# Grouped attention: values held stationary on four column strips, probabilities moving, mask as a VectorE product

## The chip, the cores and the metric

One Trainium2 chip; the program runs on one of its cores. The metric is the device time of one execution in microseconds (us), as the median of several runs. Engines are named as in the profile: PE is TensorE's matmuls and PEld its weight loads, DVE VectorE, ACT ScalarE, POOL GpSimd.

## The reference, cut to what matters

The program is a stack of feed-forward and attention layers over `x` of 8 sequences with 256 tokens and 128 channels. The change touches the second layer alone, which is two grouped attentions one after the other, a global (causal) and a local one (a window of 32 tokens), each with 16 heads of 8 channels and 4 key/value heads:

```python
def repeat_kv(x):
    return jnp.repeat(x, H // KVH, axis=1)
def sdpa(q, k, v, mask):
    scores = jnp.einsum('bhqd,bhkd->bhqk', q, k) / np.sqrt(HD).astype(np.float32)
    scores = jnp.where(mask, scores, jnp.float32(-1e+30))
    probs = jax.nn.softmax(scores, axis=-1)
    return jnp.einsum('bhqk,bhkd->bhqd', probs, v)
```

In front of it stand an RMS norm, the projections, a rotation of q and k by position and a norm of each q and k; behind it the output projection and the residual.

## The kernel before

`grouped_attention(nc, m, tag, local)` (L1145) is called twice, with tags `global` and `local`. One **unit** `n` is one sequence of 256 tokens, kept as two tiles (`PAIR`) of 128 tokens on the partitions. `threaded` (L1133) runs the eight units; each engine's queue is written out by hand in its own `unit(u, n, prev, next)`, which loops over eight **groups** `g` of two heads, and at set groups puts in a step of the unit before (`prev`, its end) or of the unit after (`next`, its start). `u` is the parity of the unit. All four queues run in order, and semaphores join them.

The steps of a unit's start, which the unit before threads through its groups:

- DVE `start_a` (L1373): statistics of the RMS norm (helper lines L109 to L119); POOL `norm_power` (L140): the power -1/2; DVE `start_b` (L1376, helper line L130): scaling.
- PE `start_a` (L1204): two transposes (L1207); ACT `start_b` (L1322): the copy to `xT`; PE `start_b`, `start_c` (L1210, L1219) with ACT `start_c` between them in the global case: the projections.
- DVE `start_d` (L1379): values to `va` (L1384), the rotation, squares and their sums (to L1397); ACT `start_d` (L1331): Ln and Exp of them; DVE `start_d2` (L1399): the norm of q and k, written as pieces of a split so that float32r products keep precision (L1403 to L1415).
- PE `start_d` (L1227): ten transposes (L1231, L1233), those of k into the bank `ps_o`; ACT `start_e` (L1337): two copies to `qT`; DVE `start_e` (L1418): the copy to `kT`.

Per group: PE `scores` (L1236) computes transposed scores of two heads into one of two buffers, keys on the partitions, queries along the free axis, as 128 x 384 columns (256 queries of the first key tile, 128 of the second; local 160 and 128). The two heads sit on different strips of 32 rows. The mask is added by a product of the identity with -30000 where masked (L1243 local, L1245 global). ACT `exps` (L1343) takes the exponentials into `pT`, which has four buffers. PE `values` (L1249) uses each head's `pT` as stationary and the values with a column of ones as moving:

```python
nc.tensor.matmul(ps_av(0, slot), p[:, 0:P], v(0), start=True, stop=True)
nc.tensor.matmul(ps_av(1, slot), p[:, W0:W], v(1), start=True, stop=local)
last = nc.tensor.matmul(ps_av(1, slot)[0:Q1, :], p[:, P:W0], v(0), start=False, stop=True, skip_group_check=local)
```

A float32 product is two records in the trace, each with its weight load. `Q1` is 128 in the global case and 32 in the local one, where L1257 is a tile of 128x32.

The end of a unit: DVE `end_a` (L1422) divides by the sums (L1424, L1427); PE `end_a` (L1262) turns the result (L1265), ACT `end_b` (L1347) copies it (L1349), PE `end_b` (L1268) projects it (L1271), DVE `end_c` (L1433) adds the residual (L1435; local also the statistics of the next norm, L109 to L121), and in the local case `residual_end` scales.

Of the kernel before, what the change touches and what calls it, by code (L numbers as in the profile page):

```python
# [17 lines left out]
P = 128  # L18
D = 128
NB = 8  # L20
SEQ = 256
# [1123 lines left out]
def grouped_attention(nc, m, tag, local):  # L1145
# [11 lines left out]
    VW = HD + 1  # L1157

    STREAM = SEQ - (HEADS - 1) * VW
    VPAD = (KV - 1) * VW + STREAM
    w = m.a0l if local else m.a0g
    src = m.H1 if local else m.XN
    with ExitStack() as ctx:
# [14 lines left out]
        ident16, hidden = (ctx.enter_context(nc.sbuf_tensor(f"{tag}_{k}", [P, w], mybir.dt.bfloat16)) for k, w in (("ident16", P), ("hidden", W)))  # L1180
        qT = sbr("qT", [P, 2, 4, SEQ])
        kT = sbr("kT", [P, 2, SEQ])
        va = sb("va", [P, 2, PAIR, VPAD])
        pT = sb("pT", [P, 4, 2, W])
        rec = sb("rec", [P, PAIR * HEADS])
        o = sb("o", [P, PAIR, HEADS, HD])
# [5 lines left out]
        s_ready, e_ready, av_ready, o_ready, otr_ready, oT_ready, y_ready = (sem(k) for k in ("s_ready", "e_ready", "av_ready", "o_ready", "otr_ready", "oT_ready", "y_ready"))  # L1192
        ps_s = lambda g: m.psum[:, 2 * (g % 2):2 * (g % 2) + 2, :]
        ps_a, ps_b = m.psum[:, 4, 0:SEQ], m.psum[:, 5, 0:PAIR * 192].rearrange("p (t f) -> p t f", t=PAIR)
        ps_av = lambda t, slot: m.psum[:, 6, 256 * t + slot * VW:256 * t + slot * VW + STREAM]
        av_heads = m.psum[:, 6, :].rearrange("p (t f) -> p t f", t=PAIR)[:, :, 0:HEADS * VW].rearrange("p t (s f) -> p t s f", f=VW)
        ps_o = m.psum[:, 7, 0:SEQ]
        ps_y = m.psum[:, 7, 256:512]
# [4 lines left out]
        def _(pe):  # L1203
# [23 lines left out]
            def start_d(u, n):  # L1227
                pe.wait_ge(qk_ready, n + 1)
                for t in range(PAIR):
# [3 lines left out]
                    last = nc.tensor.transpose(ps_o[:, t * P:(t + 1) * P], ks[:, t, :, :].rearrange("p h f -> p (h f)").bitcast(F32), m.ident[:, :])  # L1233
                last.then_inc(qkT_ready, 1)

            def scores(u, n, g):  # L1236
                for k, (kv, j) in enumerate(heads_of(g)):
                    rows = slice(4 * HD * kv, 4 * HD * (kv + 1))
                    nc.tensor.matmul(ps_s(g)[:, k, 0:W0], kT[rows, u, 0:P], qT[rows, u, j, 0:W0], start=True, stop=True)
                    nc.tensor.matmul(ps_s(g)[:, k, W0:W], kT[rows, u, P:SEQ], qT[rows, u, j, P:SEQ], start=False, stop=True, skip_group_check=True)  # L1240
                for k in range(2):
                    if local:
                        last = nc.tensor.matmul(ps_s(g)[:, k, 0:W], ident16[:, :], hidden[:, 0:W], start=False, stop=True, skip_group_check=True)  # L1243
                    else:
# [4 lines left out]
            def values(u, n, g):  # L1249
# [9 lines left out]
                if g == GROUPS - 1:  # L1259
                    last.then_inc(av_ready, 1)  # L1260
# [1044 lines left out]
```

## Time and profile before

| | us |
|---|---|
| median of 3 runs (2650.71 to 2653.58) | 2651.41 |
| the profiled execution | 2654.27 |
| its span in the profile | 2652.5 |
| busy in the span: PE 2233.1, PEld 1855.7, DVE 1509.7, ACT 1003.5, POOL 131.7 | |

Busy time is the union of an engine's instructions; matmuls are pipelined, so a record of one lasts longer than it keeps the next one waiting. Times in the rows are counted from the start of the span. "Idle before" in square brackets is how long the engine had waited, and for what. The granted clock (PEclk) is the share of TensorE's full clock in a stretch.

### The profile page before, as it was taken

How to read it: one execution, taken by the hardware profiler on the slowest of the kernel's cores; microseconds unless marked ns; L12 is line 12 of the kernel's file. 1: busy time of each engine (PE TensorE's matmuls, PEld its weight loads, DVE VectorE, ACT ScalarE, POOL GpSimd, SP SyncE). 2: the span in 40 equal slices, each digit the busy share in tenths (PEclk: the TensorE clock that was granted, in tenths of full speed). 3: DMA queues.
4: the chain of work that ended last, by engine and by line, in shares of the span. 5: the costliest groups of instructions: out<-in, count | busy, mean ns of one | idle time of the engine just before them, and what ended most of it. 6: DMA issues, size and time to landing. Idle time of an engine off the chain costs nothing. (4 is left out here: it accounts for less than half of the span.)

```text
span 2652.5 us, 41991 instructions
## 1 busy us (share of the span) xinstructions
PE 2233.1 (84%) x14884; PEld 1855.7 (70%) x14884; DVE 1509.7 (57%) x3769; ACT 1003.5 (38%) x2327; POOL 131.7 (5%) x191
## 2 busy tenths in 40 slices
PE   3588789966997788499899989999989987688885
PEld 2377666645996322399899967888779984588863
DVE  6633334366666899756632226777742238577757
ACT  2233322223222332122344435555544435344434
POOL 2100000010000100100000000000000000000000
PEclk9799989987998899599989989999989999799978
DMA  5000000000000000000000004444300000000000
GB/s 155 1 1 0 0 1 0 0 28 1 1 0 1 0 0 0 32 1 0 1 1 0 0 27 133 124 124 123 123 1 0 0 1 0 1 1 0 0 0 16
DMA packets 47122, 59.70 MB, mean 23 GB/s; under 512 B 7089, under 2 KB 44689, under 8 KB 46323
## 3 DMA queue, kind: packets, MB, share of 16 engines
q1 hardware_dynamic: 47023, 58.43, 7.2%
q8 instruction: 57, 0.93, 0.1%
q14 instruction: 42, 0.34, 0.0%
HBM read 32.20 MB, written 26.21 MB: 22 GB/s over the span
## 5 line engine op out<-in xcount | busy, mean ns | idle before, releaser
L1650 ACT ACTIVATE a_p<-psum,a_nmax 128x256 f32<-128x256 f32 x256 | 100.4, 476 | 140.1 <-DVE a_nmax L1707 140.1
L701 ACT ACTIVATE m2b_hid<-psum,m_b 128x256 f32<-128x256 f32 x256 | 100.5, 475 | 115.1 <-PE psum L55 115.0
L701 ACT ACTIVATE m2a_hid<-psum,m_b 128x256 f32<-128x256 f32 x256 | 100.5, 475 | 114.4 <-PE psum L55 114.3
L1600 PE MATMUL psum<-a_va,a_pT 128*128 128x121 f32 x1024 | 134.5, 287 | 10.9 <-DVE a_pT L1711 6.4
L1600 PEld LDWEIGHTS psum<-a_va,a_pT 128*128 128x128 f32 x1024 | 124.4, 199 | 17.7 <-DVE a_pT L1711 7.1
L686 PE MATMUL psum<-m_w,m2a_hid 128*128 128x128 f32 x1024 | 126.2, 277 | 0.0
L686 PE MATMUL psum<-m_w,m2b_hid 128*128 128x128 f32 x1024 | 126.2, 277 | 0.0
L719 DVE SCALAR_TENSOR_TENSOR m2b_acc<-psum,m2b_gates,m2b_acc 128x128 f32<-128x128 f32 x128 | 39.0, 347 | 149.2 <-PE psum L686 149.2
L719 DVE SCALAR_TENSOR_TENSOR m2a_acc<-psum,m2a_gates,m2a_acc 128x128 f32<-128x128 f32 x128 | 39.0, 347 | 148.8 <-PE psum L686 148.8
L686 PEld LDWEIGHTS psum<-m_w,m2b_hid 128*128 128x128 f32 x1024 | 122.1, 194 | 0.6
L686 PEld LDWEIGHTS psum<-m_w,m2a_hid 128*128 128x128 f32 x1024 | 122.1, 194 | 0.6
L1948 ACT ACTIVATE a_p<-a_p,a_nmax 128x256 f32<-128x256 f32 x128 | 63.9, 500 | 141.9 <-DVE a_nmax L1975 141.9
L1711 DVE COPY a_pT<-psum 128x1024 f32<-128x1024 f32 x64 | 78.3, 1224 | 64.7 <-PE psum L1587 63.6
L1056 DVE TENSOR_TENSOR_SCAN a1s_clamped<-a1s_clamp_coef,a1s_bounds 128x1024 f32<-128x1024 f32 x48 | 108.8, 2269 | 0.0
L589 ACT ACTIVATE m1b_silu<-psum 88x512 f32<-88x512 f32 x80 | 47.4, 593 | 143.7 <-PE psum L55 143.7
L589 ACT ACTIVATE m1a_silu<-psum 88x512 f32<-88x512 f32 x80 | 47.4, 593 | 143.1 <-PE psum L55 143.1
L53 PE MATMUL psum<-m1a_XT_high,m_raw_high 128*88 (+1 forms) x320 | 97.8, 306 | 0.0
L53 PE MATMUL psum<-m1b_XT_high,m_raw_high 128*88 (+1 forms) x320 | 97.4, 304 | 0.0
L1901 PE MATMUL psum<-arena,a_q 128*128 128x384 f32 x256 | 93.9, 489 | 3.1 <-ACT a_kk L1961 3.1
L55 PE MATMUL psum<-m1a_XT_high,m_raw_low 128*88 (+1 forms) x320 | 91.6, 286 | 0.0
L55 PE MATMUL psum<-m1b_XT_high,m_raw_low 128*88 (+1 forms) x320 | 91.2, 285 | 0.0
L575 PE MATMUL psum<-m_down,m1b_hid 88*128 88x128 f32 x640 | 86.5, 278 | 5.4 <-DVE m1b_hid L615 4.9
(598 smaller groups left out, 6023.2 us busy)
## 6 DMA issues: line engine op xcount, KB each, us to landing
a_scratch<-a_pos SPq DMA_DIRECT2D x64, 384.0 KB, 2.7
a_shifted<-a_scratch SPq DMA_DIRECT2D x64, 256.0 KB, 3.1
m_w<-in_m_w SPq DMA_DIRECT2D x1, 2048.0 KB
arena<-in_m_w SPq DMA_DIRECT2D x1, 2048.0 KB, 8.3
arena<-in_m_up SPq DMA_DIRECT2D x1, 1760.0 KB, 7.4
a_w<-in_a_w SPq DMA_DIRECT2D x1, 1536.0 KB, 7.9
out<-X SPq DMA_DIRECT2D x1, 1024.0 KB, 5.1
m_down<-in_m_down SPq DMA_DIRECT2D x1, 880.0 KB
```

The costliest lines, as they stand in the source:

```text
L53: nc.tensor.matmul(out, lhsT[0], rhs[0], start=True, stop=False)
L55: return nc.tensor.matmul(out, lhsT[1], rhs[0], start=False, stop=True)
L575: last = nc.tensor.matmul(ps_y(e % 2)[:, t * D:(t + 1) * D], hid[:, e % 2, k * SEQ + t * P:k * SEQ + (t + 1) * P], m.m1_down[:, e, k, :], ...
L589: nc.scalar.activation(silu[:, e % 2, :], ps_up(e % 2)[:, 0:2 * SEQ], ACT.Silu).then_inc(silu_ready, 1)
L686: last = nc.tensor.matmul(ps_y(e % 2)[:, t * D:(t + 1) * D], hid[:, e % 2, c * SEQ + t * P:c * SEQ + (t + 1) * P], m.m2_w2[:, e, c, :], st ...
L701: last = nc.scalar.activation(hid[:, e % 2, c * SEQ:(c + 1) * SEQ], ps_up(e % 2)[:, c * SEQ:(c + 1) * SEQ], ACT.Gelu, bias=m.m2_b1[:, e * ...
L719: last = nc.vector.scalar_tensor_tensor(out=a, in0=ps_y(e % 2)[:, t * D:(t + 1) * D], scalar=gates[:, t, e:e + 1], in1=a, op0=ALU.mult, op ...
L1056: nc.vector.tensor_tensor_scan(flat(clamped[:, k % RING, :, :]), flat(clamp_coef[:, k // QUARTERS % 2, :, :]), flat(bounds[:, k % RING, :, ...
L1600: last = nc.tensor.matmul(ps_av(t, 2 * g + k), pT[:, g % 4, 2 * k + kt, t * P:(t + 1) * P], va[:, u, kt, h * VW:h * VW + STREAM], start=(k ...
L1650: last = nc.scalar.activation(p[:, g % 2, k, :], ps_s(g)[:, k, :], ACT.Exp, bias=nmax[:, g % 2, k:k + 1])
L1711: nc.vector.tensor_copy(pT[:, g % 4, :, :], ps_t).then_inc(pT_ready, 1)
L1901: last = nc.tensor.matmul(ps_pos[:, t, :], q2[:, t * P:(t + 1) * P], rel_k[:, h, P - P * t:P - P * t + WIN], start=True, stop=True)
```

## The change

The mask product on PE goes. In its place DVE multiplies the exponentials by a mask of ones and zeros, in place, once a group (`mask`, new). Values become stationary: for each `j` of four (two groups, so four heads, one for each key/value head) PE runs `values(u, n, j)`, in which each of the four key/value heads has a strip of 32 columns of the array, with nine of them used, and its head's `pT` moves through. The result lies transposed, so ACT copies it out (`move_values`), PE turns it back (`turn_back`), and DVE divides it (`normalise`), four times a unit. PE `values` waits for `masked` and `av_moved`, `turn_back` for `av_moved` and `o_ready` (or `y_used`), PE `start_d` also for the second normalisation of the running unit, since k's transposes and `turn_back` share a bank. ACT `start_d` moves from group 6 to 5, ACT `start_b` and `start_c` from groups 2 and 3 to 1 and 2, DVE `start_d2` from 6 to 5, PE `end_a` and `end_b` from 1 and 2 to 2 and 3, the local `residual_end` from 4 to 5. In `scores` the order of the four products changes. The casts of identity and mask in DVE's `first` go. The diff, cut to its core:

```diff
             def start_d(u, n):
                 pe.wait_ge(qk_ready, n + 1)
+                if not isinstance(n, int) or n:
+                    pe.wait_ge(o_ready, 4 * n - 2)
...
-                for k in range(2):
-                    if local:
-                        last = nc.tensor.matmul(ps_s(g)[:, k, 0:W], ident16[:, :], hidden[:, 0:W], start=False, stop=True, skip_group_check=True)
...
-            def values(u, n, g):
-                pe.wait_ge(e_ready, GROUPS * n + g + 1)
...
+            def values(u, n, j):
+                pe.wait_ge(masked, GROUPS * n + 2 * j + 2)
+                if not isinstance(n, int) or n or j > 0:
+                    pe.wait_ge(av_moved, 4 * n + j)
+                strip = lambda kv: ps_av[STRIP * kv:STRIP * (kv + 1), :]
+                p = lambda kv: pT[:, (2 * j + kv // 2) % 4, kv % 2, :]
+                for kv in range(KV):
+                    nc.tensor.matmul(strip(kv)[:, 0:W0], va[:, u, 0, kv, :], p(kv)[:, 0:W0], start=True, stop=True)
+                for kv in range(KV):
+                    last = nc.tensor.matmul(strip(kv)[:, P:SEQ], va[:, u, 1, kv, :], p(kv)[:, W0:W], start=False, stop=True, skip_group_check=True)
+                last.then_inc(av_ready, 1)
+            def turn_back(u, n, j):
+                pe.wait_ge(av_moved, 4 * n + j + 1)
+                if j:
+                    pe.wait_ge(o_ready, 4 * n + j)
+                elif not isinstance(n, int) or n:
+                    pe.wait_ge(y_used, n)
+                for t in range(PAIR):
+                    last = nc.tensor.transpose(ps_back[:, t * P:(t + 1) * P], ov[:, j % 2, t * P:(t + 1) * P], m.ident[:, :])
+                last.then_inc(back_ready, 1)
...
             def unit(u, n, prev, next):
...
+                    if g in (2, 4, 6):
+                        values(u, n, g // 2 - 1)
+                    if g == 0 and prev:
+                        values(1 - u, n - 1, 3)
                     if next and g == GROUPS - 1:
                         pe.wait_ge(e_ready, GROUPS * n + g)
                         ready(n + 1)
                         scores(1 - u, n + 1, 0)
+                    if g in (4, 5, 7):
+                        turn_back(u, n, {4: 0, 5: 1, 7: 2}[g])
                     if prev and g == 1:
+                        turn_back(1 - u, n - 1, 3)
...
+            def move_values(u, n, j):
+                act.wait_ge(av_ready, 4 * n + j + 1)
+                nc.scalar.activation(ov[:, j % 2, :], ps_av, ACT.Copy).then_inc(av_moved, 1)
             def unit(u, n, prev, next):
                 for g in range(GROUPS):
-                    if next and g == 6:
+                    if next and g == 5:
                         start_d(1 - u, n + 1)
                     if next and g == 7:
                         start_e(1 - u, n + 1)
                     exps(u, n, g)
+                    if g in (2, 4, 6):
+                        move_values(u, n, g // 2 - 1)
+                    if prev and g == 0:
+                        move_values(1 - u, n - 1, 3)
...
+            def mask(u, n, g):
+                dve.wait_ge(e_ready, GROUPS * n + g + 1)
+                if local:
+                    p, k = pT[:, g % 4, :, :], m.window_mask[:, :].unsqueeze(1).to_broadcast([P, 2, W])
+                else:
+                    p = pT[:, g % 4, :, :].rearrange("p h (b f) -> p h b f", f=P)[:, :, 0:3:2, :]
+                    k = m.causal_mask[:, :].unsqueeze(1).unsqueeze(1).to_broadcast([P, 2, 2, P])
+                nc.vector.tensor_tensor(p, p, k, ALU.mult).then_inc(masked, 1)
+            def normalise(u, n, j):
+                dve.wait_ge(back_ready, 4 * n + j + 1)
+                back = ps_back.rearrange("p (t k f) -> p t k f", t=PAIR, f=STRIP)
+                nc.vector.reciprocal(rec[:, :, :], back[:, :, :, HD])
+                nc.vector.drain()
+                nc.vector.tensor_tensor(o[:, :, :, j, :], back[:, :, :, 0:HD], rec[:, :, :].unsqueeze(3).to_broadcast([P, PAIR, KV, HD]),
+                                        ALU.mult).then_inc(o_ready, 1)
...
             def unit(u, n, prev, next):
                 for g in range(GROUPS):
+                    mask(u, n, g)
+                    if next and g == 1:
+                        start_b(1 - u, n + 1)
+                    if prev and g == 1:
+                        normalise(1 - u, n - 1, 3)
                     if next and g == 0:
                         start_a(1 - u, n + 1)
                     if prev and g == 3:
                         end_c(1 - u, n - 1)
+                    if prev and g == 5 and local:
                         residual_end(nc, dve, m, xn, n - 1)
                     if next and g == 4:
                         start_d(1 - u, n + 1)
+                    if g == 4:
+                        normalise(u, n, 0)
+                    if next and g == 5:
+                        start_d2(1 - u, n + 1)
+                    if g == 5:
+                        normalise(u, n, 1)
+                    if next and g == 7:
+                        start_e(1 - u, n + 1)
+                    if g == 7:
+                        normalise(u, n, 2)
```

## Rows read from the trace of the kernel before

**Rows 1.** Busy time by stretch, both stages: stretch, length, busy (instructions) by engine, PEclk.

```profile
136.00:325.00 189.00, 163.85 (x1354) 138.90 (x1354) 62.10 (x240) 70.82 (x116) 4.84 (x7) 0.98 0.00 1
342.00:545.00 203.00, 188.35 (x1304) 132.19 (x1302) 71.42 (x282) 57.01 (x107) 8.99 (x13) 0.97 0.00 1
```

**Rows 2.** Instructions of L140, 160 to 460 us: count, ns, first and last start.

```profile
L140 POOL TENSOR_TENSOR global_rn_inv<-global_rn_var,neg_half x6: 690/691/692, 163.9 to 282.1; 128x2 f32<-128x2 f32 x6
...
L140 POOL TENSOR_TENSOR local_xn_inv<-local_xn_var,neg_half x4: 691/691/692, 376.4 to 452.3; 128x2 f32<-128x2 f32 x4
```

**Rows 3.** Timeline of PE, global, one group: start, length, instructions merged by line.

```profile
219.01 0.39 PE L1239 MATMUL psum<-global_qT,global_kT 32*128 32x256 f32 x2
...
219.24 0.23 PE L1240 MATMUL psum<-global_qT,global_kT 32*128 32x128 f32 x2
219.40 0.39 PE L1245 MATMUL psum<-global_hidden,global_ident 128*128 128x256 bf16 x2
219.62 0.38 PE L1255 MATMUL psum<-global_va,global_pT 128*128 128x121 f32 x2
...
220.29 0.39 PE L1255 MATMUL psum<-global_va,global_pT 128*128 128x121 f32 x2
```

**Rows 4.** Timeline of PE, local: start of a head's values, and what follows it.

```profile
441.60 0.48 PE L1255 MATMUL psum<-local_va,local_pT 128*128 128x121 f32 x2
...
442.56 0.34 PE L1239 MATMUL psum<-local_qT,local_kT 32*128 32x160 f32 x2
```

**Rows 5.** Timeline of DVE, ACT and PE, global, one unit.

```profile
200.08 0.29 DVE L1403 TENSOR_TENSOR global_qn<-global_rot,global_inv 128x128 f32<-128x128 f32 x1 [0.61 <-ACT global_inv L1335]
...
202.11 0.66 PE L1231 MATMUL psum<-ident,global_qs 128*128 128x128 f32 x4 [1.75 <-DVE global_ks L1415]
...
203.46 1.09 ACT L1340 ACTIVATE global_qT<-psum 128x512 fp32r<-128x512 f32 x2 [2.70 <-PE psum L1233]
...
208.87 0.36 DVE L1424 RECIPROCAL global_rec<-psum 128x32 f32<-128x32 f32 x1 [4.98 <-PE psum L1257]
...
209.71 0.48 DVE L109 BATCH_NORM_STATS2 global_rn_stats<-XN 128x6 f32 x2
...
211.05 0.17 DVE L119 TENSOR_SCALAR global_rn_var<-global_rn_var 128x2 f32<-128x2 f32 x1
...
211.70 0.38 ACT L1349 ACTIVATE global_oT<-psum 128x256 f32<-128x256 f32 x1 [1.32 <-PE psum L1265]
...
212.56 0.44 PE L1207 MATMUL psum<-ident,global_r 128*128 128x128 f32 x2 [0.90 <-DVE global_r L130]
...
215.63 0.42 DVE L1435 TENSOR_TENSOR global_r<-psum,XN 128x256 f32<-128x256 f32 x1 [3.13 <-PE psum L1271]
...
219.48 0.22 DVE L1384 COPY global_va<-psum 128x64 f32<-128x64 f32 x1 [2.95 <-PE psum L1224]
...
221.67 0.49 DVE L1393 TENSOR_TENSOR global_tmp<-global_rot 128x320 f32<-128x320 f32 x1
...
222.79 0.18 DVE L1397 TENSOR_SCALAR global_ss<-global_ss 128x40 f32<-128x40 f32 x1
```

**Rows 6.** Groups of instructions, ACT, both stages: count, busy us, mean ns, idle before.

```profile
L1345 ACT ACTIVATE global_pT<-psum 128x768 f32<-128x768 f32 x64 | 51.1, 809 | 46.9 <-PE psum L1245 46.9
L1345 ACT ACTIVATE local_pT<-psum 128x576 f32<-128x576 f32 x64 | 41.6, 650 | 80.2 <-PE psum L1243 79.7
```

**Rows 7.** Timeline of DVE, local, first and last instruction of `end_c`.

```profile
424.82 0.42 DVE L1435 TENSOR_TENSOR local_r<-psum,arena 128x256 f32<-128x256 f32 x1 [3.74 <-PE psum L1271]
...
426.79 0.17 DVE L121 TENSOR_SCALAR local_xn_var<-local_xn_mv 128x2 f32<-128x2 f32 x1
```

**Rows 8.** Busy time by stretch, two stretches of other stages; columns as in rows 1.

```profile
842.00:893.00 51.00, 24.71 (x86) 15.18 (x86) 34.08 (x97) 15.55 (x24) 11.07 (x12) 0.73 0.00 1
1057.00:1129.00 72.00, 32.72 (x160) 30.45 (x161) 52.34 (x190) 8.57 (x15) 12.07 (x16) 0.55 0.08 30
```

**Rows 9.** Timeline of PE, global, first unit, at the lower clock.

```profile
132.49 1.12 PE L1231 MATMUL psum<-ident,global_qs 128*128 128x128 f32 x4 [6.51 <-DVE global_ks L1415]
```

More of the change, by code:

```diff
@@ L1247, in scores @@
-                last.then_inc(s_ready, 1)
-            def values(u, n, g):
-                pe.wait_ge(e_ready, GROUPS * n + g + 1)
-                for k, (kv, j) in enumerate(heads_of(g)):
-                    slot = 2 * g + k
-                    p = pT[:, g % 4, k, :]
-                    v = lambda t: va[:, u, t, kv * VW:kv * VW + STREAM]
-                    nc.tensor.matmul(ps_av(0, slot), p[:, 0:P], v(0), start=True, stop=True)
-                    nc.tensor.matmul(ps_av(1, slot), p[:, W0:W], v(1), start=True, stop=local)
-                    last = nc.tensor.matmul(ps_av(1, slot)[0:Q1, :], p[:, P:W0], v(0), start=False, stop=True,
-                                            skip_group_check=local)
-                if g == GROUPS - 1:
-                    last.then_inc(av_ready, 1)
+                for k, rows, j in heads:
+                    last = nc.tensor.matmul(ps_s(g)[:, k, W0:W], kT[rows, u, P:SEQ], qT[rows, u, j, P:SEQ], start=True, stop=True)
@@ L1312, in tail @@
             def tail(u, n):
-                values(u, n, GROUPS - 1)
+                values(u, n, 3)
+                turn_back(u, n, 3)
                 end_a(u, n)
@@ L1364, in unit, with tail @@
                     exps(u, n, g)
+                    if g in (2, 4, 6):
+                        move_values(u, n, g // 2 - 1)
+                    if prev and g == 0:
+                        move_values(1 - u, n - 1, 3)
                     if prev and g == 2:
                         end_b(1 - u, n - 1)
-                    if next and g in (2, 3):
-                        {2: start_b, 3: start_c}[g](1 - u, n + 1)
-            threaded(act, first, unit, end_b)
+                    if next and g in (1, 2):
+                        {1: start_b, 2: start_c}[g](1 - u, n + 1)
+            def tail(u, n):
+                move_values(u, n, 3)
+                end_b(u, n)
+            threaded(act, first, unit, tail)
         @block.vector
@@ L1466, in unit @@
                         end_c(1 - u, n - 1)
-                    if prev and g == 4 and local:
+                    if prev and g == 5 and local:
                         residual_end(nc, dve, m, xn, n - 1)
```

72 lines of the change are left out of this document (23 added, 49 removed).

## The prediction

> **What bounds the kernel now.** I read the stage windows first. The change touches only the two grouped attention stages; in them TensorE (PE) is busy 163.9 of 189 us and 188.4 of 203 us, VectorE (DVE) 62 and 71, ScalarE (ACT) 71 and 57, and the granted clock is 0.98 and 0.97 [rows 1]. Then the unit, which is one sequence: GpSimd's power (L140) runs once a unit, and its first and last starts give (282.1 - 163.9) / 5 = 23.6 us for global and (452.3 - 376.4) / 3 = 25.3 us for local [rows 2]. Eight units each make the stages. Then one group of PE work: two score pairs, two mask products (0.22 us together), and per head six records of values at 0.67 us (219.62 to 220.29) [rows 3]. A local head takes 0.96 us (441.60 to 442.56) although it streams less: L1257 is a 128x32 tile there, and changing the tile shape and back costs 0.29 us a head [rows 4]. So PE bounds both stages now, and DVE and ACT wait for it.
>
> **What the change takes from PE.** Per unit the masks go (8 x 0.22 = 1.8 us) and 16 heads of values (16 x 0.67 = 10.7 us global, 16 x 0.96 = 15.4 us local). It adds per unit four blocks of values and four pairs of turning transposes. A block streams, in each strip, 2 passes x 384 columns (288 local). On a strip the next record, L1240, follows L1239's 256 columns after 0.23 us (219.01 to 219.24) [rows 3], 0.87 to 0.9 ns a column: 0.67 us global and 0.50 local if the strips run side by side, 2.7 and 2.0 if in turn. These are my two ends. I take side by side: the two L1239 records of a pair, on different row strips, together last 0.39 us, what one of 256 columns lasts, and L1240 too comes as a pair [rows 3]. With the change of shape (0.1 in, 0.1 out, from the 0.29) a block is 0.87 us to the next instruction, and its end comes a tail of some 0.17 after its last column. A turning pair is that of L1207, 0.44 us [rows 5]. PE work falls from about 20 to 12.5 us a unit in global, from 23 to 10 in local.
>
> On column strips the Trainium skill ("TensorE: Matmul & The Clock Gate", Part 3, "Measured speedup vs the span model") gives a speedup of 2.38 for three column strips, not 3. By that a global block would stream an estimated 0.85 us in place of 0.67, some 0.4 us a unit more; the sum above does not use it, and no run here shows it.
>
> **What it adds elsewhere.** Each group now has a DVE product over 512 (local 576) elements. No row has this; SBUF products take 0.29 us for 128 and 0.49 for 320 elements [rows 5], 1.04 ns an element, so 0.69 (0.76). Lower end 0.49, upper end twice that. Two instructions of normalisation replace the three of L1424 and L1427, four times a unit: between 0.22 (the copy L1384) and 0.36 (L1424) each [rows 5]; I take 0.42 with the drain. ACT gets four copies 128x256 like L1349, 0.38 each [rows 5]. The casts of the identity and mask in the setup go, two instructions a stage of the size of L1384. There are no DMAs. Reordering the score pairs costs and gains nothing: the records already start strip beside strip [rows 3].
>
> **What sets the unit then.** All queues are in order, and the preparation of the next unit is threaded through them. I walked the four queues in program order with the durations of [rows 5] and some 0.04 us a handover. Now DVE and ACT fill PE's time; afterwards the unit is one chain in which nearly every step waits for another engine. Global, from exp 0 of a unit to exp 0 of the next:
> - exp 0 (0.81 [rows 6]), mask 0 (0.62, as the next instruction starts before its end), statistics 209.71 to 211.22 (1.51), power (0.69 [rows 2] and handovers), scaling (two of 128 elements, 0.48), transposes (0.44): 4.8 us;
> - ACT: exp 2, exp 3 and between them four copies (xT in front, values 0, oT, latent) of 0.4 to 0.5 each, like L1349: 3.3, at 8.1;
> - DVE: mask 3, end_c (L1435, a copy as large and their drains, 0.9), mask 4, start_d 219.48 to 222.98 (3.5): 5.7, at 13.8. start_d's input is there 1.3 us before; the masks and end_c stand in front of it;
> - ACT: Ln and Exp of the norm (L1403 waits 0.61 us for them), then exp 5 behind them: 1.4, at 15.1;
> - DVE: mask 5, start_d2 200.08 to 202.1 (2.0), normalisation 1, for which PE's start_d now waits: 3.1, at 18.3;
> - PE: ten transposes, 202.11 until L1340 starts at 203.46 (1.3), values 2: 2.2, at 20.5;
> - ACT: the copy of values 2, the two qT copies 1.09, exp 7 behind them: 2.2, at 22.7;
> - DVE: mask 7, and kT behind it: 1.1; PE: the next scores: 0.6. Total 24.4 us [rows 5].
>
> So the waits that PE's load hid are the bound next. Local is the same with exp at 0.65 [rows 6], masks of 0.76, an end_c of 2.1 us (424.82 to 426.96) [rows 7] and the residual's end in front of start_d2, but no latent copy: 25.1 us. At full clock the unit changes by +0.8 and -0.2 us: the 9 to 13 us taken from PE buy nothing. The last unit of a stage has no next one to prepare and PE closes it now; with the setup it saves 2 us global and 7 local. Seven pitches each: 7 x 0.8 - 2 + 7 x (-0.2) - 7 = -5 us.
>
> **The clock.** PE would be busy (tails included) 13.3 of 24.4 us and 11.1 of 25.1, so 55% and 44%. Stretches like that: 48% busy (24.7 of 51) with clock 0.73, 45% (32.7 of 72) with 0.55, against 0.98 at 87% [rows 1, 8]. The granted clock has two levels, 1.2 and 2.4 GHz; at the lower one four of the transposes last 1.12 us, not 0.66 [rows 5, 9]. The same walk with every PE step doubled gives 30.3 and 30.1 us a unit (+5.9, +5.0). I take 0.77 for global, by its 55% between the rows of 48% and 87% (46% of the time at the lower level: +2.7 us a unit), and 0.65 for local, between 0.55 and 0.73 (70%: +3.5): 7 x 6.2 = +43 us.
>
> The skill's rule in the same page (Part 1, "What's actually happening") is that the throttled state is the default and activity releases it. It speaks against a change that empties PE. Rows 8 agree; without it the sum would end at -5.
>
> **The sum.** 2654.3 us (the profiled execution; span 2652.5 and 1.8 around it) - 5 + 43 = 2692. That execution lies 2.9 us above the median of 2651.4, so I forecast 2690.
>
> **Rivals.**
> 1. The clock holds at the higher level: 2651.4 - 5 = 2646. For it: the gaps come one by one between dense groups, and in global PE stays over half busy. Against: rows 8.
> 2. The strips run in turn. A block takes 2.0 (1.5) us more, two of four blocks lie on the chain and one delays exp 1; the walk gives 29.9 and 28.8 us a unit, +64 us over case 1, and with a part of the clock's loss about 2745. For it: no row shows column strips beside each other. Against: the row strips.
> 3. The lower level nearly throughout: -5 + 7 x 10.9 + some 10 at the ends: 2730.
> 4. Faster: the DVE queue's load, not the handovers, sets the unit. Its place is start_d to start_d2 in groups 4 and 5: if that preparation runs beside exps 3 to 6 and not between them, 3.5 to 5.5 us a unit go, 14 x 4.5 = 63 us: about 2590. It decides once the pitch is under 23.6 and 25.3. For it: DVE's work is only 14 to 15 us a unit (62.1 / 8 or 71.4 / 8 [rows 1], and 8 masks plus 1 more). Against: exp 5 stands behind ACT's wait for start_d, and kT behind mask 7.
>
> **How the numbers follow.** Forecast 0.58 (2665 to 2725), case 1 0.12, case 2 0.10, case 3 0.05, case 4 0.15. A mask at 0.49 or 0.98 moves five steps a unit, -14 or +20 us, which is in these bounds. No change means within 0.2%, 5 us, about what can be measured. Faster: case 4 and half of case 1, 0.21; same: the rest of case 1, 0.06; slower 0.73. The range 2632 to 2740 leaves out case 4 and part of case 2.
>
> **What would show it.** Pitch by L140: 27 and 28.5 us. PE idle before its start_d transposes, DVE idle at masks 3, 5 and 7, ACT idle before exp 2 and exp 5. Clock 0.6 to 0.8 in both stages. In a block four records starting within a few ns say side by side; one after the other is case 2. I am wrong if the pitches are under 23.6 and 25.3, or the clock stays over 0.95.

## The result and the profile after

The changed kernel takes 2719.42 us (median of 4 runs, 2715.54 to 2719.59) against 2651.93 for the kernel before beside it: a ratio of 1.0256, 95% interval 1.0243 to 1.0269. It is 68 us slower; forecast were 2690 us and a range of 2632 to 2740. The profiled execution has a span of 2717.2 us, 65 more than before, and the two attention stages hold 60 of them: from the first power (L140) of a stage to the first of the next one, global lasts 244.8 us (207.1 before) and local 244.9 (222.5). Some 4 us lie behind the two stages, in work that the change does not touch (2108.2 us against 2103.8).

The stage windows, the same stretches and columns as [rows 1]:

```profile
136.00:325.00 189.00, 130.49 (x866) 78.72 (x866) 92.42 (x298) 65.18 (x124) 5.21 (x7) 0.56 0.00 0
342.00:545.00 203.00, 113.96 (x824) 75.53 (x824) 107.86 (x350) 57.52 (x120) 10.23 (x12) 0.55 0.00 0
```

TensorE's busy time fell from 163.9 to 130.5 us and from 188.4 to 114.0, and the granted clock from 0.98 and 0.97 to 0.56 and 0.55: the lower level for nearly nine tenths of the time. The unit, by the starts of L140 as in [rows 2]:

```profile
L140 POOL TENSOR_TENSOR global_rn_inv<-global_rn_var,neg_half x6: 691/691/692, 167.8 to 312.1; 128x2 f32<-128x2 f32 x6
...
L140 POOL TENSOR_TENSOR local_rn_inv<-local_rn_var,neg_half x6: 690/928/1245, 408.3 to 556.8; 128x2 f32<-128x2 f32 x6
```

That is 144.3 / 5 = 28.9 us for global and 148.5 / 5 = 29.7 us for local, in place of 23.6 and 25.3. The new operations, as groups by line (count | busy us, mean ns | idle before):

```profile
L1445 DVE TENSOR_TENSOR local_pT<-local_pT,window_mask 128x576 f32<-128x576 f32 x64 | 48.5, 758 | 69.3 <-ACT local_pT L1349 67.2 <-issue 1.7
L1445 DVE TENSOR_TENSOR global_pT<-global_pT,causal_mask 128x512 f32<-128x512 f32 x64 | 44.2, 690 | 88.2 <-ACT global_pT L1349 86.5 <-issue 1.6
...
L1248 PE MATMUL psum<-global_pT,global_va 128*32 128x256 f32 x256 | 33.7, 619 | 0.8 <-DVE global_pT L1445 0.7
...
L1353 ACT ACTIVATE global_ov<-psum 128x256 f32<-128x256 f32 x32 | 12.3, 385 | 93.0 <-PE psum L1250 93.0
...
L1452 DVE TENSOR_TENSOR global_o<-psum,global_rec 128x64 f32<-128x64 f32 x32 | 7.2, 225 | 2.4
...
L1450 DVE RECIPROCAL global_rec<-psum 128x8 f32<-128x8 f32 x32 | 6.5, 204 | 13.7 <-PE psum L1260 13.6
```

The mask takes 0.69 and 0.76 us, the copy 0.385, the two instructions of a normalisation 0.20 and 0.23. L1248's 256 records last 0.619 us each, 158 us together, in 33.7 us of busy time: more than four at once. In a block the four strips start 6 to 7 ns apart (285.856, 285.862, 285.869 and 285.876 us); they run side by side.

One unit of the global stage, from exponential 0 to the next (timeline; the rows at which the prediction's steps end, the waits that it named, and one block of values, L1248 and L1250, up to the instruction behind it):

```profile
279.66 0.81 ACT L1349 ACTIVATE global_pT<-psum 128x768 f32<-128x768 f32 x1 [1.70 <-PE psum L1238]
...
284.62 0.69 PE L1202 MATMUL psum<-ident,global_r 128*128 128x128 f32 x2 [1.09 <-DVE global_r L130]
...
285.35 0.47 ACT L1328 ACTIVATE global_xT<-psum,a0g_norm 128x256 f32<-128x256 f32 x1 [1.90 <-PE psum L1202]
...
285.86 1.08 PE L1248 MATMUL psum<-global_pT,global_va 128*32 128x256 f32 x8
...
286.71 0.65 PE L1250 MATMUL psum<-global_pT,global_va 128*32 128x128 f32 x8
...
287.29 0.69 PE L1266 MATMUL psum<-ident,global_o 128*128 128x128 f32 x2
...
289.29 1.48 ACT L1349 ACTIVATE global_pT<-psum 128x768 f32<-128x768 f32 x2
...
290.11 0.69 DVE L1445 TENSOR_TENSOR global_pT<-global_pT,causal_mask 128x512 f32<-128x512 f32 x1 [2.86 <-ACT global_pT L1349]
...
293.16 0.23 DVE L1400 COPY global_va<-psum 128x64 f32<-128x64 f32 x1 [0.52 <-PE psum L1219]
...
296.49 0.18 DVE L1413 TENSOR_SCALAR global_ss<-global_ss 128x40 f32<-128x40 f32 x1
...
296.70 0.24 ACT L1337 ACTIVATE global_inv<-global_ss 128x40 f32<-128x40 f32 x1 [1.68 <-DVE global_ss L1413]
...
297.15 1.49 ACT L1349 ACTIVATE global_pT<-psum 128x768 f32<-128x768 f32 x2
...
297.98 0.69 DVE L1445 TENSOR_TENSOR global_pT<-global_pT,causal_mask 128x512 f32<-128x512 f32 x1 [0.86 <-ACT global_pT L1349]
...
300.74 0.22 DVE L1452 TENSOR_TENSOR global_o<-psum,global_rec 128x64 f32<-128x64 f32 x1
...
301.02 1.12 PE L1228 MATMUL psum<-ident,global_qs 128*128 128x128 f32 x4 [2.33 <-DVE global_o L1452]
...
304.92 0.38 ACT L1353 ACTIVATE global_ov<-psum 128x256 f32<-128x256 f32 x1 [6.27 <-PE psum L1250]
...
307.01 0.69 DVE L1445 TENSOR_TENSOR global_pT<-global_pT,causal_mask 128x512 f32<-128x512 f32 x1 [5.45 <-ACT global_pT L1349]
...
308.91 0.81 ACT L1349 ACTIVATE global_pT<-psum 128x768 f32<-128x768 f32 x1 [1.93 <-PE psum L1238]
```

Here every step of the prediction's walk can be read. Exponential 0 starts at 279.66; the transposes of `r` end at 285.31, after 5.65 us (4.8 forecast); exponential 3, the first of the two merged at 289.29, ends at 290.1: 4.8 more (3.3); start_d ends at 296.67: 6.6 (5.7); exponential 5 near 297.96: 1.3 (1.4); normalisation 1 at 300.96: 3.0 (3.1); the ten transposes and values 2 until the copy starts at 304.92: 4.0 (2.2); exponential 7, with mask 7 at 307.01: 2.1 (2.2); kT, the scores and the next exponential 0 at 308.91: 1.9 (1.7). The fourth, fifth and seventh step, with DVE and ACT work alone, last what was forecast; the excess of 4.8 us lies in the steps that TensorE takes part in or holds up, and its four transposes of L1228 last 1.12 us, as in [rows 9], and not 0.66. In the third step DVE waits 0.52 us for the projection (L1219), so the input of start_d was not early, as forecast. In the first, mask 0 begins at 281.09, 0.62 us after the end of exponential 0, with the normalisation of values 2 ahead of it (until 280.79), which the walk does not list. The waits that the prediction named as signs are all there: TensorE 2.33 us ahead of its start_d, DVE 2.86, 0.86 and 5.45 at masks 3, 5 and 7, ACT 1.90 at the copy ahead of exponential 2 and 1.68 at the norm ahead of exponential 5.

### The profile page after: what moved, and what is told of

It reads as the page before. It is cut to its first block and busy times, and to the rows that moved or that the text cites. A ratio compares the mean times of both kernels' runs of the same rounds, so it can differ in the third digit from the quotient of the medians.

```text
span 2717.2 us, 41374 instructions
## 1 busy us (share of the span) xinstructions
PE 2173.7 (80%) x14244; PEld 1770.4 (65%) x14244; DVE 1604.7 (59%) x3973; ACT 1019.0 (38%) x2391; POOL 134.0 (5%) x191
## 5 line engine op out<-in xcount | busy, mean ns | idle before, releaser
L1445 DVE TENSOR_TENSOR global_pT<-global_pT,causal_mask 128x512 f32<-128x512 f32 x64 | 44.2, 690 | 88.2 <-ACT global_pT L1349 86.5
```

## The experiments

All stand against the kernel before, timed beside them on the same chip: its median was 2651.5 us beside runs 1 to 4, 2659.2 beside 5 to 8 and 2651.1 beside 9 to 12, so runs of different chips are compared by their ratios. Unit and clock are those of the profiled execution (in run 8 it was 8 us under the median). The unit is taken from five intervals of L140 in each stage (in the local stage three in the first row, where five give 25.6, and four in the row of run 11), the clock from the stretches 160 to 270 us (global) and 345 to 440 us (mostly local). Behind the two stages, in work that no run touches, the profiled executions differ by up to 20 us (2096.4 in run 5, 2116.9 in run 3).

| run | us | ratio to before (95%) | us a unit, global / local | clock |
|---|---|---|---|---|
| before | 2651.9 | 1 | 23.6 / 25.3 | 1.00 / 0.99 |
| after | 2719.4 | 1.0256 (1.0243 to 1.0269) | 28.9 / 29.7 | 0.59 / 0.54 |
| 1 TensorE kept busy | 2689.7 | 1.0140 (1.0112 to 1.0168) | 26.7 / 28.2 | 0.75 / 0.73 |
| 2 wait without mask | 2689.1 | 1.0135 (1.0106 to 1.0165) | 27.5 / 27.4 | 0.57 / 0.52 |
| 3 mask on TensorE | 2653.1 | 1.0010 (0.9994 to 1.0027) | 23.1 / 25.4 | 0.77 / 0.63 |
| 4 exponential 7 first | 2688.0 | 1.0136 (1.0108 to 1.0164) | 27.1 / 28.2 | 0.57 / 0.55 |
| 5 old values, VectorE mask | 2685.4 | 1.0105 (1.0086 to 1.0124) | 26.5 / 27.3 | 0.89 / 0.75 |
| 6 reordered | 2598.9 | 0.9768 (0.9752 to 0.9785) | 20.7 / 22.2 | 0.67 / 0.61 |
| 7 reordered, mask on TensorE | 2566.7 | 0.9645 (0.9626 to 0.9664) | 17.4 / 21.4 | 0.95 / 0.83 |
| 8 reordered, kept busy | 2583.6 | 0.9715 (0.9699 to 0.9731) | 18.6 / 20.0 | 0.95 / 0.86 |
| 9 before, reordered | 2619.5 | 0.9871 (0.9844 to 0.9897) | 20.2 / 22.9 | 1.00 / 1.00 |
| 10 as 7, local kept busy | 2583.2 | 0.9740 (0.9718 to 0.9763) | 17.1 / 22.9 | 0.97 / 0.75 |
| 11 as 8, power beside a normalisation | 2572.1 | 0.9697 (0.9674 to 0.9720) | 17.6 / 20.7 | 1.00 / 0.86 |
| 12 strip by strip | 2723.7 | one run | 29.1 / 29.9 | 0.52 / 0.52 |

### 1. Is it the clock? TensorE kept busy

```diff
+            def keep_busy(bank, count):
+                for _ in range(count):
+                    nc.tensor.transpose(m.psum[:, bank, 0:P], m.ident[:, :], m.ident[:, :])
...
+                    if next and g == 5:
+                        keep_busy(4, 12)
                     if g in (4, 5, 7):
                         turn_back(u, n, {4: 0, 5: 1, 7: 2}[g])
```

(the other three places alike: ahead of `start_d`, of `ready(n + 1)`, and 8 ahead of `start_a`)

> The changed kernel with 44 transposes of the identity more on TensorE in each unit (8, 12, 12 and 12 of them), whose results nothing reads, put where its queue stands waiting; nothing else is touched. At full clock 12 of them last 1.3 us, less than each of the waits they stand in (1.5 to 3.3 us in the trace). Theory A (the unit is a chain of handovers that at full clock would last 24.4 and 25.1 us, and what makes it 29.1 and 29.7 is the clock alone): clock over 0.9 in both stages in place of 0.56 and 0.55, pitch 24.4 to 25.5, so 2719 - 7 x 4.5 - 7 x 4.4 = about 2657 us (2645 to 2670). Rival B (the loss lies in the new operations and handovers themselves, the low clock only goes with it): the pitch stays over 28 us whatever the clock, 2710 us or more, since TensorE has more to do.

TensorE has more to do and the kernel is 30 us faster. The stage windows of this run:

```profile
136.00:325.00 189.00, 164.63 (x1238) 117.82 (x1235) 99.61 (x319) 70.15 (x134) 7.67 (x7) 0.72 0.00 1
345.00:560.00 215.00, 154.88 (x1234) 118.10 (x1234) 121.93 (x396) 63.66 (x135) 12.96 (x14) 0.72 0.00 0
```

The clock rose to 0.72 only, not over 0.9, so the time stopped between the two forecasts. TensorE's timeline shows where it was won and lost (line numbers of this run; L1281 are the added transposes):

```profile
229.39 0.58 PE L1236 MATMUL psum<-global_qT,global_kT 32*128 32x256 f32 x2
...
230.01 2.72 PE L1281 MATMUL psum<-ident 128*128 128x128 f32 x12
...
232.88 0.38 PE L1236 MATMUL psum<-global_qT,global_kT 32*128 32x256 f32 x2
...
233.25 1.53 PE L1281 MATMUL psum<-ident 128*128 128x128 f32 x12
...
240.74 0.39 PE L1236 MATMUL psum<-global_qT,global_kT 32*128 32x256 f32 x2 [1.88 <-DVE global_kT L1446]
...
242.31 0.40 PE L1250 MATMUL psum<-global_pT,global_va 128*32 128x128 f32 x8
242.64 0.53 PE L1236 MATMUL psum<-global_qT,global_kT 32*128 32x256 f32 x2
```

Twelve transposes at 230.01 take 2.72 us, the lower level; from 232.5 on the clock is up, the score pair L1236 goes from 0.58 to 0.38 us and the next twelve take 1.53. At 242.64, after a stretch with a wait of 1.88 us, scores, strips and one turning back, the pair is back at 0.53. In the first half of the unit TensorE's queue is full of projections, scores and strips (busy for all of the 8 us from 222 to 230) and the granted clock is 0.50 throughout. The size fits: the prediction's walk lies at 24.4 us at full clock and 30.3 at the lower one; at 0.59 that makes 24.4 + 0.82 x 5.9 = 29.2 (measured 28.9), at 0.75 it makes 27.3 (26.7); local 29.7 (29.7) and 27.8 (28.2). Theory A holds in kind, though its 2657 us needed a clock that did not come, and rival B, 2710 us or more, is out. The 30 us are what is left after GpSimd's power, which takes 1.06 to 1.17 us in 14 of this run's 16 units and 0.69 in most units of the changed kernel (see 11).

### 2 and 3. The mask: its work, or its place in the queue?

```diff
-                nc.vector.tensor_tensor(p, p, k, ALU.mult).then_inc(masked, 1)
+                dve.sem_inc(masked, 1)
```

> The changed kernel without the multiplication by the mask: VectorE waits for each exponential as it did and then only raises the signal, so the order of every queue stays. The mask is left out of the computation. Theory A (five of the eight masks, 0, 3, 4, 5 and 7, lie on the chain, 0.62 us of VectorE each): 3.1 us a unit less in both stages, 14 x 3.1 = 43: about 2676 us (2660 to 2690), the clock little changed. Rival C (VectorE's masks fill time in which it would wait anyway): 2710 to 2720 us.

(The mask is left out of the computation.) 30 us faster, not 43, and certainly not nothing. The 43 were worked out at full clock. Worked out after the run, the same walk with TensorE's steps doubled gives 1.9 and 2.7 us a unit for it, 32 us: by the walk, TensorE ends last in more places at the lower clock, and a shorter VectorE step is worth less there.

Run 3 takes the product with `hidden` back into `scores`, drops `mask` from VectorE's loop and lets the values wait for the exponentials:

```diff
-                    mask(u, n, g)
...
-                pe.wait_ge(masked, GROUPS * n + 2 * j + 2)
+                pe.wait_ge(e_ready, GROUPS * n + 2 * j + 2)
```

> The changed kernel with the mask of the kernel before: the identity times the hidden entries on TensorE ahead of the exponential, no mask in VectorE's queue; the strips, the copies, the turning back and the rest of the order stay. Theory A: not only the multiplications leave the chain (3.1 us) but also VectorE's waits for the exponentials ahead of start_d, start_d2 and the copy of kT, another 1.5 us or so at full clock; TensorE has 1.8 us a unit more and would be busy in two thirds of a unit, so the clock rises to 0.75 or more: pitch 20 to 23 us, 2719 - 14 x 7.5 = about 2615 us (2585 to 2640), faster than both kernels. Rival C (the strips and their handovers are the loss, wherever the mask stands): 2690 us or more. Rival B (only VectorE's work counts, not its place in the queue): as the run without the multiplication, about 2676.

66 us faster than the change, twice what the multiplications alone are worth. The other half is VectorE's waits for the exponentials in front of `start_d`, `start_d2` and kT together with a higher clock (0.77 and 0.63 against 0.59 and 0.54); no run separates the two. But not faster than before, which had been expected. Its windows:

```profile
160.00:270.00 110.00, 86.81 (x702) 52.71 (x702) 44.55 (x181) 45.92 (x90) 3.16 (x5) 0.77 0.00 0
345.00:440.00 95.00, 73.52 (x548) 46.60 (x546) 39.61 (x166) 31.52 (x68) 4.13 (x6) 0.63 0.00 1
```

The clock did reach 0.77 in global, but 0.63 in local, and TensorE carries more of the unit: the walk of this kernel, made after the run, is 19.7 us at full clock and 29.2 at the lower one (local 20.7 and 28.0), which at these clocks makes 24.0 and 26.1 (measured 23.1 and 25.4). The expectation had taken the clock's rise without the larger price of each step below it. Strips alone, then, leave the total as it was: by the walk, the work they save comes back as clock. In the profiled execution the two stages are 10 us shorter than before (207.6 and 212.2 us against 207.1 and 222.5), and the untouched work behind them is 13 us longer; why was not followed.

### 4. One place in one queue

```diff
-                    if next and g == 7:
-                        start_e(1 - u, n + 1)
                     exps(u, n, g)
-                    if g in (2, 4, 6):
-                        move_values(u, n, g // 2 - 1)
+                    if g in (2, 4, 7):
+                        move_values(u, n, {2: 0, 4: 1, 7: 2}[g])
+                    if next and g == 7:
+                        start_e(1 - u, n + 1)
```

> The changed kernel with one place in ScalarE's queue changed: exponential 7 goes ahead of the copy of values 2 and of the two copies of qT, in place of behind them. No instruction is added or taken. Theory A (the order of the queues sets the unit): mask 7 and behind it the copy of kT no longer wait for exponential 7; 1.8 us a unit less at full clock, so 14 x 1.8 = 25: about 2694 us (2675 to 2700). Rival C (the time lies in the operations, and another wait takes its place): 2714 to 2722 us.

2688.0 us: 1.8 and 1.5 us a unit, with the clock as low as before. The order of a queue is worth as much as the whole multiplication.

### 5. The other half alone

The kernel before with `mask` in VectorE's loop, `values` waiting for it, and no product with `hidden`; its values are the old ones.

> The kernel before with one half of the change: the mask moves from TensorE to VectorE (the same multiplication, ahead of everything else in each group, and the values wait for it), while the values stay as they were, probabilities stationary and no strips. Theory A (neither half is dear by itself; only both together empty TensorE so far that its clock falls): TensorE is still busy 18 of 24 us a unit, the clock stays over 0.9, and a walk of the queues gives 24.3 and 25.9 us a unit against 23.3 and 25.3 for the kernel before: 2651 + 7 x 1.0 + 7 x 0.6 = about 2662 us (2652 to 2685). Rival B (the multiplications on VectorE and their handovers are the loss): most of the 68 us of the change is there, 2690 us or more.

```profile
160.00:270.00 110.00, 87.51 (x647) 77.81 (x646) 55.31 (x166) 37.22 (x63) 4.41 (x4) 0.89 0.00 1
345.00:440.00 95.00, 73.56 (x414) 52.57 (x414) 49.45 (x157) 23.09 (x44) 5.53 (x6) 0.75 0.00 1
```

A ratio of 1.0105, 28 us, between the two forecasts: the mask on VectorE does cost something by itself, and the clock did not stay over 0.9 with it. The walk had 24.3 and 25.9 us a unit at full clock; measured are 26.5 and 27.3, with the clock at 0.89 and 0.75 and GpSimd's power at 1.10 us and not 0.69 (see 11). With the strips at 1.0010 the halves would add up to 30 us; together they cost 68. In the two stages of the profiled executions the mask costs 38 us, the strips save 10, and both together cost 60. So about half of the loss is there only when both halves are. By the walk they share a chain (at full clock 23.3 us a unit before, 19.7 with strips, 24.3 with the mask, 24.4 with both, in global); and they share a clock.

### 6. The same instructions in another order

The loops of the three queues are written as a list (`+` is the unit after, `-` the one before; k mask, n normalise, e exponential, m copy of values, s scores, v values, t turn back):

```diff
+TensorE: "s1 v3- s2 t3- s3 start_a+ s4 end_a- start_b+ end_b- start_c+ v0 s5 t0 v1 t1 s6 s7 start_d+ v2 scores+ t2"
+ScalarE: "e0 e1 m3- e2 start_b+ end_b- start_c+ e3 m0 start_d+ e4 m1 e5 e6 e7 start_e+ m2"
+VectorE: "start_a+ k0 start_b+ n3- k1 k2 end_c- k3 start_d+ n0 start_d2+ n1 k4 k5 residual- start_e+ k6 k7 n2"
```

> The changed kernel with the same instructions in another order on TensorE, ScalarE and VectorE: on VectorE the statistics of the next unit ahead of mask 0, its start_d right behind mask 3 and start_d2 ahead of masks 4 and 5, the copy of kT ahead of masks 6 and 7; on ScalarE exponentials 5 to 7 ahead of the copies of qT; on TensorE values later and the transposes ahead of values 2. Theory A (the order of the queues, not the work, sets the unit): a walk of the queues gives 17.1 and 18.5 us a unit at full clock and 24.3 and 23.3 with TensorE at half; with a clock of 0.7 some 21.4 us in both stages, 2719 - 7 x 7.7 - 7 x 8.3 = about 2607 us (2560 to 2640), faster than both kernels. Rival C (other waits take the place of those removed): 2680 us or more. Rival B (the new operations are the loss): 2700 or more.

A ratio of 0.9768: 129 us under the change (0.0488 of 2652) and 2.3% under the kernel before, with no instruction added or taken; the two stages of the profiled execution are 116 us shorter than the change's (373.7 us against 489.7). Windows, and L140 in the global stage:

```profile
160.00:270.00 110.00, 95.56 (x700) 59.57 (x700) 74.29 (x242) 53.23 (x100) 5.58 (x5) 0.67 0.00 0
345.00:440.00 95.00, 63.97 (x519) 44.80 (x519) 69.77 (x232) 37.28 (x79) 7.49 (x8) 0.61 0.00 0
```

```profile
L140 POOL TENSOR_TENSOR global_rn_inv<-global_rn_var,neg_half x6: 1113/1118/1122, 157.5 to 261.2; 128x2 f32<-128x2 f32 x6
```

With these clocks the walk makes 21.9 and 22.2 us (measured 20.7 and 22.2). Theory A was right in size; B and C are out.

### 7 and 8. Order and clock together

Run 7 is run 3 in such an order (values 2 and 1 earlier, no masks on VectorE).

> Strips with the mask on TensorE as in the kernel before, and the queues in an order like that of the reordered run (exponentials and values of a group later than the next unit's preparation). Theory A: a walk of the queues gives 16.7 and 18.8 us a unit at full clock, 28.1 and 26.2 with TensorE at half; since TensorE now has 14 of 17 us to do the clock should stay higher, 0.8 or more: 20 to 21.5 us a unit, 2719 - 14 x 8.5 = about 2600 us (2545 to 2640). Rival C (TensorE's work bounds again and the order buys nothing over the run with the mask on TensorE alone): 2640 to 2660.

```profile
160.00:270.00 110.00, 95.85 (x968) 61.48 (x960) 55.57 (x230) 65.32 (x122) 4.13 (x6) 0.95 0.00 1
345.00:440.00 95.00, 66.83 (x655) 45.66 (x654) 50.70 (x211) 39.04 (x84) 6.20 (x9) 0.83 0.00 0
```

2566.7 us, the fastest of the study: 3.5% under the kernel before, 6.0% under the change by the ratios. The clock is 0.95 in global, where 17.4 us a unit stand against the walk's 16.7, and 0.83 in local.

Run 8 is run 6 with transposes put into TensorE's queue (`b`, with their number; the diff is against run 6):

```diff
-"... s3 start_a+ ... v1 t1 s6 ..."
+"... s3 b6+ start_a+ ... v1 b20+ t1 s6 ..."
```

> The reordered run with 26 transposes of the identity more on TensorE in each unit, results unread: 6 ahead of the transposes of r and 20 ahead of turning back values 1, where TensorE would wait 0.8 and 3 to 4 us. Theory A (what is left over the walk at full clock is the clock): the clock rises by 0.1 or more over that of the reordered run, and the time falls by 10 to 35 us against it, towards 7 x 17.1 and 7 x 18.5 us. Rival D (at that order TensorE's own work bounds, and more of it costs): 5 us or more slower than the reordered run.

```profile
160.00:270.00 110.00, 97.75 (x947) 67.45 (x946) 83.47 (x269) 60.55 (x115) 5.58 (x5) 0.95 0.00 1
```

Useless work again buys time: the clock went from 0.67 to 0.95, and 15 us went against run 6, timed on the same chip.

### 9. The control: does order alone do it?

> The control for the reordered runs: the kernel before, its work unchanged, with its three queues reordered in the same manner (VectorE's end_a, end_c and start_d of the next unit early, ScalarE's exponentials 5 and 6 ahead of the norm, TensorE's transposes ahead of the last values). Theory A (before the change TensorE's own work bounds, so order can give back only the few us in which TensorE waits): a walk of the queues gives 19.6 and 22.9 us a unit against 23.0 and 25.1, 7 x 3.4 + 7 x 2.2 = 39 us, a ratio of 0.985 to the kernel before; the reordered forms of the change (0.965 to 0.977) stay ahead of it, because they have 8 to 13 us a unit less for TensorE. Rival E (the gain of the reordered runs is order alone, and the change adds nothing to it): a ratio of 0.975 or less. Rival F (TensorE has no gaps to give back): 0.995 to 1.005.

```profile
160.00:270.00 110.00, 110.00 (x933) 95.97 (x932) 46.28 (x178) 48.70 (x83) 3.44 (x5) 1.00 0.00 1
345.00:440.00 95.00, 95.00 (x692) 68.97 (x690) 41.96 (x168) 30.37 (x59) 5.54 (x9) 1.00 0.00 1
```

A ratio of 0.9871, as the walk said (20.2 and 22.9 us measured, 19.6 and 22.9 forecast). Rivals E and F are out. TensorE is busy for all of both stretches at full clock: this order leaves no gap that another could fill (whether another order of TensorE's own products would be shorter was not tried). The reordered change lies below it by 1 to 2.3%; that this is so because it has less for TensorE to do is argued from the work, not tried apart. So the change is worth having, once the queues are arranged for it, though the 2.3% are those of run 7, which has only the strips and leaves the mask on TensorE.

### 10 and 11. Two details

> The reordered run with the mask on TensorE, and in the local stage 24 transposes of the identity more in each unit, results unread, ahead of turning back values 1, where TensorE waits some 4 us. Theory A (in local 20.4 us a unit stand against 18.8 of the walk because the clock is lower for a third of each unit): the local clock rises from 0.83 to 0.9 or more and 5 to 12 us go: a ratio to the kernel before of about 0.961. Rival D (the transposes only delay): the same time or up to 15 us more.

```profile
345.00:440.00 95.00, 80.60 (x671) 57.24 (x670) 44.13 (x185) 33.99 (x72) 5.51 (x8) 0.75 0.00 0
```

A miss: by the ratios 25 us slower than run 7, and the local clock fell, to 0.75. Of the 25 us the profiled executions show 10 in the local stage (191.0 us against 181.0), the only one that was touched. So the outcome is rival D's in size, but its reason, that the transposes delay, is not what the trace shows:

```profile
L1311 PE MATMUL psum<-ident x168: 272/273/273, 303.1 to 441.0; 128*128 128x128 f32 x168
```

All 168 last 0.27 us, as at full clock, 24 of them take 2.78 us in each of the seven units, in a place where run 7 waits 4.8 to 5.2 us in six of the seven, and in six TensorE still waits 1.7 to 2.6 us behind them. What differs is the clock after them: in four units the lower level then lasts 13.7 to 17.1 us in a row, against 6.8 us in most units of run 7. Why, and whether that makes the 10 us, is open.

> The reordered and kept busy run with one move in VectorE's queue: the normalisation of values 3 stands between the statistics and the scaling, where mask 0 stood, and mask 0 behind the scaling. In the reordered run GpSimd's power lasted 1.11 to 1.19 us in 12 of 14 units, and 0.69 where no mask was running when it began. Theory G (GpSimd's power waits until the mask product that is already running on VectorE has ended; a normalisation, with one source in PSUM, doesn't hold it): the power lasts 0.69 us again, 0.3 to 0.5 us a unit off the chain, 4 to 6 us in all against the run it is derived from. Rival H (the power is slowed by whatever VectorE does beside it): it stays over 0.9 us, and the time stays the same.

In run 6 a mask product was already running when the power began; in run 11 a normalisation runs in that place (timelines, one unit each):

```profile
157.39 0.69 DVE L1442 TENSOR_TENSOR global_pT<-global_pT,causal_mask 128x512 f32<-128x512 f32 x1
...
157.50 1.12 POOL L140 TENSOR_TENSOR global_rn_inv<-global_rn_var,neg_half 128x2 f32<-128x2 f32 x1 [20.86 <-DVE global_rn_var L119]
...
158.66 0.48 DVE L130 TENSOR_SCALAR global_r<-XN,global_rn_inv 128x128 f32 x2 [0.58 <-POOL global_rn_inv L140]
```

```profile
157.14 0.69 POOL L140 TENSOR_TENSOR global_rn_inv<-global_rn_var,neg_half 128x2 f32<-128x2 f32 x1 [19.89 <-DVE global_rn_var L119]
...
157.87 0.48 DVE L130 TENSOR_SCALAR global_r<-XN,global_rn_inv 128x128 f32 x2 [0.26 <-POOL global_rn_inv L140]
```

The power is back at 0.69 us in every unit, and VectorE waits 0.26 us for it and not 0.58. In run 6 the power ended 0.54 us after the mask did (158.62 against 158.08); in all five slow ones of the changed kernel it was 0.55 us after. Theory G holds for the duration: the power waits for the product to end. The Trainium skill says so ("SBUF — State Buffer", "Summary: rules for kernel authors"): a VectorE instruction with two SBUF inputs and a GpSimd one that reads SBUF exclude each other, and the second to issue waits for the first to finish. The trace agrees where the power is the second; where the mask is the second it does not show the wait: a mask that began 0.13 us after a power of the changed kernel (225.86 us) lasted its 0.69 us all the same. The longer power also stands in runs 1, 4 and 5 (1.06 to 1.24 us in 14, 12 and 14 of 16 units), and part of what they cost or gained is that. For the total, 0.9697 against 0.9715, the intervals overlap: a gain of 5 us was forecast and is not established (one execution of each has 4 us less in the two stages, 342.8 against 347.1).

### 12. Strip by strip

```diff
                 for kv in range(KV):
                     nc.tensor.matmul(strip(kv)[:, 0:W0], va[:, u, 0, kv, :], p(kv)[:, 0:W0], start=True, stop=True)
-                for kv in range(KV):
                     last = nc.tensor.matmul(strip(kv)[:, P:SEQ], va[:, u, 1, kv, :], p(kv)[:, W0:W], start=False, stop=True, skip_group_check=True)
```

> The changed kernel with the eight matmuls of a block of values issued strip by strip (both passes of strip 0, then both of strip 1, and so on) in place of the first passes of all four strips and then the second. The work is the same. Theory A (strips run side by side only where neighbours in the queue are on different strips, since TensorE issues in order): only the second pass of one strip lies beside the first of the next, a block takes four first passes and one second, at the lower clock 4 x 0.43 + 0.22 = 1.9 us in place of 0.65; two blocks lie on the chain, so 2.5 us a unit or more, 2755 us or more. Rival I (a matmul that waits for its strip doesn't hold up the strips behind it): 2715 to 2725 us, the four first passes still within a few ns.

```profile
L1248 PE MATMUL psum<-global_pT,global_va 128*32 128x256 f32 x256 | 34.8, 627 | 0.8 <-DVE global_pT L1444 0.7
```

The first passes still overlap as in the changed kernel (34.8 us busy for 256 records of 0.627), 13 ns apart instead of 6 to 7, and the time is 2723.7 us, in a single run. Rival I is right, by the trace above all.

## Why the prediction was right, and where its size was off

- **What bounds it now, and what PE loses.** Right. TensorE was the bound ([rows 1]; run 9 shows it at its end). The strips run side by side, against rival 2, and the block takes 1.43 us to the next instruction at the lower level (285.86 to 287.29 above) and 0.79 at the higher one, in run 7; 0.87 was forecast:

```profile
237.51 0.64 PE L1268 MATMUL psum<-global_pT,global_va 128*32 128x256 f32 x8
...
238.30 0.39 PE L1251 MATMUL psum<-global_qT,global_kT 32*128 32x256 f32 x2
```

By the Trainium skill's speedup of 2.38 for three column strips ("TensorE: Matmul & The Clock Gate", Part 3, "Measured speedup vs the span model") a block would take an estimated 1.05 us, with 0.85 of streaming in place of 0.67. Run 7's 0.79 us does not agree with it.

- **The added operations.** Mask 0.69 and 0.76, copy 0.38, normalisation 0.43 with its two instructions, all as forecast.
- **The chain of handovers.** Right in the main (timeline above): the steps with DVE and ACT work alone within 0.1 us, and the waits as named. Two readings were off: start_d's input came 0.5 us late and not 1.3 early, and the normalisation of values 2 ahead of mask 0 was left out. Runs 4 and 6 show that it is the order: moving instructions alone gives 31 and 129 us. Rival 4, faster if the preparation runs beside the exponentials, named the right place; it needed the queues to be rearranged, which the change does not do.
- **The clock.** This is the mis-sized term. "I take 0.77 for global ... and 0.65 for local" rested on the busy share of other stretches [rows 8]; granted were 0.56 and 0.55. With the walk's own two ends that is 7 x (28.9 - 27.1) + 7 x (29.7 - 28.6) = 20 of the 29 us between 2690 and 2719; of the other 9, some 4 lie behind the two stages, 2 at their ends, and 2.5 come of going from profiled executions to medians. Busy share was a poor scale. TensorE is busy 69% of the global stretch at 0.56, while [rows 8] had 48% busy at 0.73. In run 1 it is busy all the time from 222 to 230 us, at the lower level; the clock rises at 232.5, behind 2.5 us of transposes, and falls again in a stretch in which TensorE is busy for 2.27 of 3.5 us (239.5 to 243). The outcome lies inside the bounds given to the forecast (2665 to 2725), but nearest to rival 3, the lower level throughout (2730), which had been given 0.05; rival 1 fell with the clock. No run held the higher level in this order of the queues, so the -5 us at full clock remains a figure of the walk.
- **What was missed.** That GpSimd's power could be held up by a mask (0.4 to 0.6 us in one of seven global units and four of seven local ones here). And that the halves interact: the prediction summed chain and clock, but did not say that either half alone leaves TensorE full enough to keep much of its clock (0.77 and 0.63 in run 3, 0.89 and 0.75 in run 5).

## What to carry to other kernels

When a change takes work from the engine that bounds a stage, redo the order of the other queues with it: the same instructions had a ratio of 1.026 in one order and of 0.977 in another. Walk the in-order queues for a unit at both clock levels; weighted by the measured clock, the two walks gave the unit of the changed kernel and of runs 1, 3 and 6 to 8 within 1.2 us. The clock itself they do not give; no walk here forecast it. And judge it by what TensorE ran in stretches with a known clock, not by its busy share: a stretch of projections, scores and strips was busy throughout and stood at the lower level (run 1).

## What the runs showed of the hardware that was not expected

- Useless transposes make the kernel faster: 44 a unit gave 30 us (run 1), 26 a unit 15 us (run 8). But 24 a unit in the local stage, in a wait that was long enough for them, went with a local stage 10 us longer (run 10).
- A matmul that has to wait for its strip does not hold up those behind it on other strips: issued strip by strip, the first passes of the four still start 13 ns apart (run 12).
- GpSimd's power (0.69 us) ends about 0.55 us after a VectorE product of two SBUF operands that was running when it began, 1.06 to 1.25 us in all in the changed kernel; a product begun later leaves it at 0.69, and is not held up by it either (0.69 us for a mask begun 0.13 us after the power).
